# First cross-attention of a two-layer decoder: the totals of two chunk sums taken by TensorE's accumulation instead of by GpSimd

## The chip, the cores and the metric

The kernel runs on one core of a Trainium2 chip. The metric is the device time of one execution in microseconds (us), smaller is better. The profile names the engines PE (TensorE's matmuls), PEld (its weight loads), DVE (VectorE), ACT (ScalarE), POOL (GpSimd) and SP (SyncE, which issues the DMAs). All engines run their own instruction streams in order and meet at semaphores.

## The reference, cut to what matters

The whole program is a decoder of two layers (each: a mixer or self-attention, a cross-attention over a context, a feed-forward with experts), with a layer norm after each part. The change touches only the cross-attention of the first layer: 2 batch rows, 256 queries and 512 context rows each, 16 heads of 64.

```python
# inside _L0_xattn_ref: b = 2, n = 256, s = 512, HEADS = 16, DHEAD = 64
q = (lat @ Wq).reshape(b, n, HEADS, DHEAD).transpose(0, 2, 1, 3)
...
k = apply_rope(k, cos[None, None], sin[None, None])
scale = DHEAD ** (-0.5)
attn = jnp.einsum('bhnd,bhsd->bhns', q, k) * scale
attn = jnp.clip(attn, -11.0, 11.0)
attn = jax.nn.softmax(attn, axis=-1)
out = jnp.einsum('bhns,bhsd->bhnd', attn, v)
out = out.transpose(0, 2, 1, 3).reshape(b, n, INNER)
return out @ Wo + bo
```

So each head and query needs a denominator: the sum over 512 context rows of the clipped exponentials.

## The kernel before, in words

The attention is worked off in 16 entries p = 2c + b, where c (0 to 7) is a pair of heads and b (0 or 1) a batch row. In an entry, context rows lie on the partitions; they come as 4 tiles of 128, taken two at a time, so an entry has two chunks s = 0 and 1, numbered n = 4c + 2b + s (32 in all). The logits of a chunk fill two PSUM banks (128 x 1024); ScalarE takes the exponential (L907) into one of four places `ex(n)`, VectorE clips it in place (L1298, `e0_clip`), and then two engines read it: TensorE multiplies it with the values (`mix0`, into the left half of bank 4 + b, `e0_used`) and GpSimd adds the two context tiles of the chunk (L703) into `esum[:, s, :]` (`e0_sum`). After the second chunk GpSimd adds the two sums into `etot[:, b, :]` (L710, `e0_tot`). `denominators0` on TensorE multiplies the total with a block of ones, two products of 64 columns by 256, one for each head of the pair, into the right half of bank 4 + b, which adds over the partitions (`o0_ps`). VectorE takes the reciprocal of it (L1290) and multiplies (L1291, `o0_norm`).

The order is written out by hand. In iteration p, TensorE does a projection (and, for b = 0, one half of a later key product; for b = 1 only the other half), then the logits of entry p + 1, the mix of entry p, and the denominators of entry p - 1. On VectorE, the two clips of an entry stand ahead of the reciprocal of the entry two before (`normed0(c - 1, b)`), then, for b = 1, the two products of a rotary step (L1236). On GpSimd the sums of an entry stand ahead of its total, and after b = 1 comes `rotated0` (L664), which finishes keys that TensorE needs some entries later. The waits that matter: the mix of entry p waits for `o0_norm` of entry p - 2 (same PSUM half), ScalarE's exponential of chunk n waits for `e0_used` and `e0_sum` of chunk n - 4 (same place in `ex`), GpSimd's first sum of an entry waits for the total before (`e0_tot`, since `esum` has one place for each s), and GpSimd's total waits for `o0_ps` of the entry two before (since `etot` has one place for each b). The last chunk (n = 31) has no sum on GpSimd: `last_denominators0` reads `esum` and the exponentials themselves.

All matmuls go through the helper `mm`, so they all stand on L1676; the tile names tell them apart (`ps<-big` is the denominators, and in the first entries the logits; `ps<-big,late` the mix, `ps<-big,mid` the logits from entry 3 on). Each float32 product shows as two records in the profile.

Of the kernel before, what the change touches and what calls it, by code (L numbers as in the profile page):

```python
# [25 lines left out]
B, T = 2, 256  # L26
# [45 lines left out]
def program(nc, a, out):  # L72
    f32, bf16, u8 = mybir.dt.float32, mybir.dt.bfloat16, mybir.dt.uint8
    ALU, ACT, AX = mybir.AluOpType, mybir.ActivationFunctionType, mybir.AxisListType
    ctx = ExitStack()
    with ctx:
# [3 lines left out]
        def sem(name):  # L80
            return ctx.enter_context(nc.semaphore(name))
# [65 lines left out]
        def rv4(name):  # L147
# [48 lines left out]
        ones_sb = big2(3700, [P, PARTS * H * B * CS // P], bf16)  # L196
        ones_col = sb("ones_col", [P, 1])
        half_x = [big1(4096 * half, [P, 4096])[64:P] for half in range(2)]
        late_hidden, first_hidden = big1(2048, [P, 2048])[64:P], big1(0, [P, 2048])[64:P]
        cxT = ctx_r(2048, [P, B * CS])  # L200
# [9 lines left out]
        esum = big2(1536, [P, 2, 2 * T])  # L210
        etot = big2(2560, [P, 2, 2 * T])
        ones0 = big2(3584, [P, DH0])
# [43 lines left out]
        ps = ctx.enter_context(nc.psum_tensor("ps", [P, 8, 512], f32))  # L256
# [30 lines left out]
        S = {k: sem(k) for k in (  # L287
            "w1_ps", "v1_ps", "x1p_done", "conv_done", "xc_done", "gate_done",
            "dt_ps", "z_done", "BC_ps", "BC_done", "lg_done", "delta_parts", "dx_parts",
            "delta_done", "delta_rest", "second_quads", "late_quads",  # L290
            "spread_d", "spread_x", "dA_done", "dBx_done", "scan_done", "hC_done", "y_ps",
            "yv_done", "mo_ps", "res_ready", "x2_done", "ff_ps", "ff_act", "ff2_ps",
            "cxnT_ps", "cxnT_done",
            "k0_ps", "k0_mul", "k0_done", "q0_ps", "q0_done", "v0_ps", "v0_done", "s0_ps", "e0_exp",
            "e0_clip", "e0_used", "e0_sum", "e0_tot", "o0_ps", "o0_norm", "y0_ps",
# [120 lines left out]
        def before_in_bank(L, slot):  # L416

            placed = placed_slots(L)
            at = [s for _, s, _ in placed].index(slot)
            same = [s for n, s, bank in placed[:at] if bank == placed[at][2]]  # L420
            return same[-1] if same else None
# [61 lines left out]
        def ex(n):  # L483

            return ex_last if n % 4 == 3 else ex_first[:, n % 4, :]

        def half(t, b):

            return t[:, b * NJ // B:(b + 1) * NJ // B, :].rearrange("p j d -> p (j d)")
# [32 lines left out]
        def stack_x(sp, half):  # L522

            heads = slice(HB * half, HB * half + HB)
            sp.wait_ge(S[f"x_zero{half}"], 2 - half)
            for c in range(PARTS * PARTS):
                sp.dma_start(ks["x"][DH * c:DH * c + DH, heads, :],
                             scr_kx[P // 2 * half:P // 2 * half + P // 2, c // PARTS, :]
                             .rearrange("(h d) t -> d h t", d=DH)).then_inc(S["x_stack"], 16)
            sp.dma_start(ks["x"][STACK:ROWS, heads, :], ones_rows[:, heads, :]  # L530
                         ).then_inc(S["x_stack"], 16)
# [84 lines left out]
        def _(pool):  # L616
# [43 lines left out]
            def rotated0(n):  # L660

                c, b = divmod(n, B)
                pool.wait_ge(S["k0_mul"], 2 * n + 2)
                nc.gpsimd.tensor_tensor(kT0[c][:, b * CS:(b + 1) * CS], kt1[n % 2], kt2[n % 2],  # L664
                                        ALU.add).then_inc(S["k0_done"], 1)
# [27 lines left out]
            for n in range(4 * NPAIR):  # L693
                c, u = divmod(n, 4)
                b, s = divmod(u, 2)

                if n == 4 * NPAIR - 1:
                    continue
                pool.wait_ge(S["e0_clip"], n + 1)
                if n >= 2:  # L700
                    pool.wait_ge(S["e0_tot"], 2 * c + b)
                e = ex(n).rearrange("p (r k t) -> p r k t", r=2, k=2)
                nc.gpsimd.tensor_tensor(esum[:, s, :].rearrange("p (r t) -> p r t", r=2),  # L703
                                        e[:, :, 0, :], e[:, :, 1, :], ALU.add
                                        ).then_inc(S["e0_sum"], 1)
                if s == 1:
                    pool.wait_ge(S["e0_sum"], n + 1)
                    if c:
                        pool.wait_ge(S["o0_ps"], 2 * (c - 1) + b + 1)
                    nc.gpsimd.tensor_tensor(etot[:, b, :], esum[:, 0, :], esum[:, 1, :], ALU.add  # L710
                                            ).then_inc(S["e0_tot"], 1)
                if u == 3 and K_FIRST + c < B * NPAIR:
                    rotated0(K_FIRST + c)
            root("post1")
# [959 lines left out]
        def _(pe):  # L1674
            def mm(o, lhsT, rhs, start=True, stop=True, shared=False):
                return nc.tensor.matmul(o, lhsT, rhs, start=start, stop=stop, skip_group_check=shared)  # L1676
# [161 lines left out]

            def denominators0(c, b):

                pe.wait_ge(S["e0_tot"], 2 * c + b + 1)
                for r in range(2):
                    ins = mm(ps[64 * r:64 * r + 64, 4 + b, T:2 * T], ones0,
                             etot[:, b, r * T:(r + 1) * T], False, True, True)
                ins.then_inc(S["o0_ps"], 1)

            def last_denominators0(parts):

                n, b = 4 * NPAIR - 1, B - 1
                pe.wait_ge(S["e0_sum"], n)  # L1850
                for part in parts:
                    for r in range(2):
                        rhs = (esum[:, 0, r * T:(r + 1) * T] if part == 0 else
                               ex(n)[:, r * 512 + (part - 1) * T:r * 512 + part * T])
                        ins = mm(ps[64 * r:64 * r + 64, 4 + b, T:2 * T], ones0, rhs, False, part == 2, True)
                return ins
# [17 lines left out]
            for p in range(B * NPAIR):  # L1874
                c, b = divmod(p, B)
# [13 lines left out]
                if p + 1 < B * NPAIR:  # L1889
                    pe.wait_ge(S["k0_done"], p + 2)  # L1890
                    if b:
                        pe.wait_ge(S["q0_done"], c + 2)
                    logits0(2 * p + 2)
                    logits0(2 * p + 3)
                    mix0(2 * p)
                    mix0(2 * p + 1)
                    if p:
                        denominators0(*divmod(p - 1, B))
                else:
                    output0(2)  # L1900
                    output0(3)
                    denominators0(c, 0)
                    output0(4)
                    mix0(2 * p)
                    last_denominators0((0,))
                    mix0(2 * p + 1)
                    last_denominators0((1, 2)).then_inc(S["o0_ps"], 1)
# [14 lines left out]
            for i in range(2):  # L1922
                for k in range(4):
                    t = 4 * i + k
                    ins = mm(ps[:, 7 - 4 * i, k * P:(k + 1) * P], cxT[:, t * P:(t + 1) * P],
                             w_x1[:, 2, :])
# [8 lines left out]
            for j in range(NJ):  # L1935
                ins = mm(ps[:, 4, j * E0:(j + 1) * E0], xT[:, j * P:(j + 1) * P], w_r0[:])
# [566 lines left out]
```

## Time and profile before

| | us |
|---|---|
| median of 3 timed runs | 450.51 (449.87 to 451.18) |
| the profiled execution, whole time | 447.8 |
| its span (first to last instruction) | 446.0 |
| of the span, PE busy | 407.5 |
| DVE busy | 303.2 |
| ACT busy | 205.1 |
| POOL busy | 196.5 |

The first cross-attention's entries lie between about 88 and 185 us of the span. A row of the timeline gives the start, the duration, the engine, the source line, what is written and read, and how many instructions are merged; an idle time ahead of it stands in brackets with what ended it. The chain of work that ended last follows back from the last instruction to whatever released each step.

### The profile page before, as it was taken

The page shows a single profiled execution, that of the slowest core. Times are in us where ns is not written, and L with a number is a line of the kernel's source. Part 1 is how long each engine was busy: PE and PEld are TensorE (multiplying, and loading weights), DVE is VectorE, ACT ScalarE, POOL GpSimd, SP SyncE. Part 2 cuts the span into 40 slices and gives each one's busy share as a digit, 9 for nine tenths or more (in the row PEclk, how much of TensorE's full clock was granted, in tenths as well). Part 3 has the DMA queues.
Part 4 walks back from the last instruction along what each step waited for, and adds up shares of the span by engine and source line. Part 5 has one row for each costly group of instructions (what it writes and reads, how often), then busy time and mean ns, then how long its engine had stood idle before and what let it go on. Part 6 is the DMA issues. An engine that isn't in the chain of part 4 may idle for free.

```text
span 446.0 us, 7698 instructions
## 1 busy us (share of the span) xinstructions
PE 407.5 (91%) x2882; PEld 275.8 (62%) x2882; DVE 303.2 (68%) x688; ACT 205.1 (46%) x290; POOL 196.5 (44%) x237
## 2 busy tenths in 40 slices
PE   4898999999999999989999986799779999999985
PEld 4576644455555557747898764445555555558974
DVE  4779976768988888624424978573798894355654
ACT  1676633154333333242333476457256545557550
POOL 3316657699988887050322556212453233000000
PEclk9989999999999999999999998899999999999999
DMA  8812000000005111350251015100000000010000
GB/s 299 320 33 85 2 1 1 1 1 0 1 0 190 48 47 48 100 193 1 103 77 22 2 31 69 15 3 3 0 2 3 2 3 2 2 37 1 0 1 24
DMA packets 8080, 19.78 MB, mean 44 GB/s; under 512 B 1958, under 2 KB 3974, under 8 KB 7526
## 3 DMA queue, kind: packets, MB, share of 16 engines
q1 hardware_dynamic: 8044, 19.30, 14.6%
q8 instruction: 23, 0.38, 0.3%
q14 instruction: 13, 0.11, 0.1%
HBM read 17.26 MB, written 1.15 MB: 41 GB/s over the span
## 4 chain that ended last, share of the span: by engine, by line
PE 72%; DVE 14%; DMA 5%; issue 3%; POOL 3%; ACT 3%; SPq 0%; DVEq 0%; POOLq 0%; ACTq 0%
PE ps L1676 70%; DMA late<-mid 4%; DVE ps L1421 3%; DVE big L1227 2%; DVE ps L1222 2%; DVE mx_a L1425 1%; PE ps L1688 1%; DMA ident<-in_ident 1%; DVE big L1298 1%; POOL rstd L638 1%; POOL big L657 1%; PE ps L2150 1%; PE ps L2073 0%; ACT late L1073 0%; DVE mid L1451 0%
## 5 line engine op out<-in xcount | busy, mean ns | idle before, releaser
L1676 PE MATMUL ps<-big,late 128*32 128x256 f32 (+3 forms) x768 | 96.1, 380 | 3.2 <-DVE mx_a L1425 1.5
L967 ACT ACTIVATE big<-ps 128x1024 f32<-128x1024 f32 x48 | 49.0, 1023 | 39.5 <-PE ps L1676 39.3
L1676 PE MATMUL ps<-late,big 128*128 128x128 f32 (+1 forms) x448 | 65.6, 277 | 1.5 <-DMA late<-mid 1.5
L1676 PEld LDWEIGHTS ps<-big,late 128*32 128x32 f32 (+2 forms) x768 | 36.7, 116 | 38.1 <-issue 14.9
L1676 PEld LDWEIGHTS ps<-late,big 128*128 128x128 f32 (+1 forms) x448 | 47.2, 152 | 19.7 <-issue 12.9
L636 POOL TENSOR_SCALAR vareps<-meanvar 128x2 f32<-128x2 f32 (+2 forms) x13 | 2.9, 226 | 110.0 <-DVE meanvar L1121 106.2
L907 ACT ACTIVATE big<-ps 128x1024 f32<-128x1024 f32 x32 | 31.0, 1022 | 38.9 <-PE ps L1676 37.5
L1421 DVE CUSTOM_DVE_ANT_0 ps<-ps,big 128x512 f32<-128x512 f32 x64 | 42.7, 708 | 6.9 <-PE ps L1676 5.8
L703 POOL TENSOR_TENSOR big<-big 128x512 f32<-128x512 f32 x31 | 43.8, 1428 | 5.5 <-DVE big L1298 5.3
L1298 DVE TENSOR_SCALAR big<-big 128x1024 f32<-128x1024 f32 x32 | 36.4, 1159 | 13.2 <-ACT big L907 12.8
L929 ACT ACTIVATE big<-ps 128x512 f32<-128x512 f32 x32 | 19.1, 597 | 36.7 <-PE ps L1676 36.7
L1676 PE MATMUL ps<-ident 128*128 128x128 f32 x182 | 27.5, 296 | 5.9 <-DMA ident<-in_ident 5.8
L1676 PE MATMUL ps<-ctx_r,attn_w 128*128 128x512 f32 x64 | 31.8, 607 | 0.7 <-ACT late L874 0.7
L1676 PEld LDWEIGHTS ps<-ident 128*128 128x128 f32 x182 | 25.5, 211 | 7.4 <-DMA ident<-in_ident 5.8
L1290 DVE RECIPROCAL big<-ps 128x256 f32<-128x256 f32 x16 | 28.0, 1748 | 3.0 <-PE ps L1676 3.0
L1676 PE MATMUL ps<-attn_w,ctx_r 128*128 128x128 f32 (+1 forms) x192 | 29.6, 288 | 0.3 <-ACT late L980 0.3
L1676 PE MATMUL ps<-xT,late 128*128 128x256 f32 (+1 forms) x96 | 29.6, 451 | 0.0
L657 POOL TENSOR_TENSOR big<-big,mid 128x512 f32<-128x512 f32 x16 | 20.4, 1273 | 19.5 <-DVE big L1227 19.5
L1676 PEld LDWEIGHTS ps<-attn_w,ctx_r 128*128 128x128 f32 (+1 forms) x192 | 23.8, 170 | 7.7 <-issue 2.9
L755 POOL CAST mid<-mid 4x256 bf16<-4x256 f32 (+1 forms) x12 | 4.6, 387 | 50.5 <-ACT mid L1023 50.4
L1425 DVE TENSOR_REDUCE mx_a<-ps 128x2 f32<-128x512 f32 x32 | 20.4, 685 | 8.8 <-PE ps L1676 8.8
L1676 PE MATMUL ps<-attn_w,big 128*128 128x128 f32 x192 | 25.4, 278 | 0.6 <-DVE big L1633 0.6
(261 smaller groups left out, 754.4 us busy)
## 6 DMA issues: line engine op xcount, KB each, us to landing
attn_w<-in_w_x SPq DMA_DIRECT2D x1, 2560.0 KB, 13.6
big<-parts_kx SPq DMA_DIRECT2D x18, 128.0 KB
late<-in_w_up SPq DMA_DIRECT2D x1, 2048.0 KB, 7.8
late<-in_w_dn SPq DMA_DIRECT2D x4, 512.0 KB, 3.8
attn_w<-in_w_up SPq DMA_DIRECT2D x1, 1024.0 KB, 7.9
attn_w<-in_w_dn SPq DMA_DIRECT2D x1, 1024.0 KB, 10.1
big<-mid SPq DMA_DIRECT2D x24, 32.0 KB, 1.8
parts_kx<-ctx_r SPq DMA_DIRECT2D x1, 768.0 KB, 3.2
```

The costliest lines, as they stand in the source:

```text
L657: nc.gpsimd.tensor_tensor(hC[:, s % 8, :], hs[:, s % 4, :], Cn[:], ALU.mult).then_inc(S["hC_done"], 1)
L703: nc.gpsimd.tensor_tensor(esum[:, s, :].rearrange("p (r t) -> p r t", r=2), e[:, :, 0, :], e[:, :, 1, :], ALU.add).then_inc(S["e0_sum"], 1)
L907: nc.scalar.activation(ex(n).rearrange("p (r n) -> p r n", r=2), ps[:, 2 * (n % 2):2 * (n % 2) + 2, :], ACT.Exp).then_inc(S["e0_exp"], 1)
L929: nc.scalar.activation(dst, ps[:, up_bank0(k, c), :], ACT.Gelu).then_inc(S["up0_act"], 1)
L967: nc.scalar.activation(ex1[:, n % 3, :].rearrange("p (r n) -> p r n", r=2), ps[:, 2 * (n % 2):2 * (n % 2) + 2, :], ACT.Exp, scale=scale).t ...
L1222: nc.vector.tensor_tensor(dBx, dBx, Bn[:], ALU.mult).then_inc(S["dBx_done"], 1)
L1227: nc.vector.tensor_tensor_scan(hs[:, s % 4, :], dA[:, s % 2, :], dBx, 0.0, ALU.mult, ALU.add).then_inc(S["scan_done"], 1)
L1290: link(nc.vector.reciprocal(dst, ps[:, 4 + b, T:2 * T]))
L1298: nc.vector.tensor_scalar(ex(n), ex(n), float(np.exp(CLIP)), float(np.exp(-CLIP)), ALU.min, ALU.max).then_inc(S["e0_clip"], 1)
L1421: nc.vector.tensor_tensor_reduce(ps[:, bank, :], ps[:, bank, :], mq[:, 2 * b + q, :], 1.0, -FAR, ALU.add, ALU.max, dst).then_inc(S[f"{L}_r ...
L1425: nc.vector.tensor_reduce(dst, ps[:, bank, :].rearrange("p (h k) -> p h k", h=heads), AX.X, ALU.max).then_inc(S[f"{L}_redmax"], 1)
L1676: return nc.tensor.matmul(o, lhsT, rhs, start=start, stop=stop, skip_group_check=shared)
```

## The change

GpSimd makes no totals any more. The two arrays `esum` and `etot` become one place of two sums for each batch row: entry (c, b) writes its sum s to `esum[:, s, :]` when b = 0 and to `etot[:, s, :]` when b = 1 (the helper `sums0`). GpSimd's sums wait for `o0_ps` of the entry two before in place of `e0_tot`, both sums of an entry and not the total alone. `denominators0` waits for `e0_sum` in place of `e0_tot`, and issues four products in place of two: it accumulates the two sums in PSUM. The last entry's handling only changes the name of the place.

```diff
+        def sums0(b, s):
+
+            return (esum, etot)[b][:, s, :]
...
                 pool.wait_ge(S["e0_clip"], n + 1)
-                if n >= 2:
-                    pool.wait_ge(S["e0_tot"], 2 * c + b)
+                if c:
+                    pool.wait_ge(S["o0_ps"], 2 * (c - 1) + b + 1)
                 e = ex(n).rearrange("p (r k t) -> p r k t", r=2, k=2)
-                nc.gpsimd.tensor_tensor(esum[:, s, :].rearrange("p (r t) -> p r t", r=2),
+                nc.gpsimd.tensor_tensor(sums0(b, s).rearrange("p (r t) -> p r t", r=2),
                                         e[:, :, 0, :], e[:, :, 1, :], ALU.add
                                         ).then_inc(S["e0_sum"], 1)
-                if s == 1:
-                    pool.wait_ge(S["e0_sum"], n + 1)
-                    if c:
-                        pool.wait_ge(S["o0_ps"], 2 * (c - 1) + b + 1)
-                    nc.gpsimd.tensor_tensor(etot[:, b, :], esum[:, 0, :], esum[:, 1, :], ALU.add
-                                            ).then_inc(S["e0_tot"], 1)
...
             def denominators0(c, b):
 
-                pe.wait_ge(S["e0_tot"], 2 * c + b + 1)
-                for r in range(2):
-                    ins = mm(ps[64 * r:64 * r + 64, 4 + b, T:2 * T], ones0,
-                             etot[:, b, r * T:(r + 1) * T], False, True, True)
+                pe.wait_ge(S["e0_sum"], 4 * c + 2 * b + 2)
+                for s in range(2):
+                    for r in range(2):
+                        ins = mm(ps[64 * r:64 * r + 64, 4 + b, T:2 * T], ones0,
+                                 sums0(b, s)[:, r * T:(r + 1) * T], False, s == 1, True)
                 ins.then_inc(S["o0_ps"], 1)
```

TensorE's stream in the middle of the attention, before: the mix of an entry (`big,late`), the denominators of the entry before (`big`), the key product, and the next logits.

```order
180 L1676 MATMUL ps<-big,late 64x256 [waits e0_clip]
181 L1676 MATMUL ps<-big,late 64x256 x3
182 L1676 MATMUL ps<-big 64x256 [waits e0_tot]
183 L1676 MATMUL ps<-big 64x256
184 L1676 MATMUL ps<-ctx_r,attn_w 128x512 [waits q0_done]
185 L1676 MATMUL ps<-big,mid 128x256 [waits e0_exp,q0_done,k0_done]
```

And the same stretch now:

```order
180 L1674 MATMUL ps<-big,late 64x256 [waits e0_clip]
181 L1674 MATMUL ps<-big,late 64x256 x3
182 L1674 MATMUL ps<-big 64x256 [waits e0_sum]
183 L1674 MATMUL ps<-big 64x256 x3
184 L1674 MATMUL ps<-ctx_r,attn_w 128x512 [waits q0_done]
185 L1674 MATMUL ps<-big,mid 128x256 [waits e0_exp,q0_done,k0_done]
```

Nothing is moved on TensorE; the denominators are four products where they were two, and wait for another semaphore.

GpSimd's stream in the entries of one pair of heads, before (L703 the sums, L710 the totals, L664 the rotary step):

```order
50 L703 TENSOR_TENSOR big<-big 128x512 [waits e0_tot,e0_clip] x2
51 L710 TENSOR_TENSOR big<-big 128x512 [waits o0_ps,e0_sum]
52 L703 TENSOR_TENSOR big<-big 128x512 [waits e0_tot,e0_clip] x2
53 L710 TENSOR_TENSOR big<-big 128x512 [waits o0_ps,e0_sum]
54 L664 TENSOR_TENSOR mid<-dtmp 128x512 [waits k0_mul]
```

And now (L707 the sums, L668 the rotary step), from the rotary step ahead of them:

```order
46 L668 TENSOR_TENSOR mid<-dtmp,big 128x512 [waits k0_mul]
47 L707 TENSOR_TENSOR big<-big 128x512 [waits o0_ps,e0_clip] x4
48 L668 TENSOR_TENSOR mid<-dtmp 128x512 [waits k0_mul]
49 L707 TENSOR_TENSOR big<-big 128x512 [waits o0_ps,e0_clip] x4
50 L668 TENSOR_TENSOR mid<-dtmp,big 128x512 [waits k0_mul]
```

The totals are gone, the four sums of a pair stand in one run, and each now waits for `o0_ps`, which the totals alone did.

## Rows read from the trace of the kernel before

**Rows 1.** The page: span, busy time of each engine.
```profile
span 446.0 us, 7698 instructions
PE 407.5 (91%) x2882; PEld 275.8 (62%) x2882; DVE 303.2 (68%) x688; ACT 205.1 (46%) x290; POOL 196.5 (44%) x237
```
**Rows 2.** Chain that ended last, in order of time, 88 to 187 us.
```profile
87.85 15.94 PE ps L1676 x102
...
103.81 1.03 ACT big L907
...
104.87 3.28 DVE big L1298 x2
108.16 1.68 DVE big L1290
...
109.86 0.43 DVE big L1291
...
110.42 76.39 PE ps L1676 x544
```
**Rows 3.** Who waited for whom: engine PE, 88 to 187 us.
```profile
PE ps L1676 <- DVE big L1291: 0.5, 1, 0.5
```
**Rows 4.** Groups by line and shape, 90 to 186 us.
```profile
L703 POOL TENSOR_TENSOR big<-big 128x512 f32<-128x512 f32 x31 | 43.8, 1428 | 5.5 <-DVE big L1298 5.3
L1298 DVE TENSOR_SCALAR big<-big 128x1024 f32<-128x1024 f32 x32 | 36.4, 1159 | 13.2 <-ACT big L907 12.8
L1290 DVE RECIPROCAL big<-ps 128x256 f32<-128x256 f32 x16 | 28.0, 1748 | 3.0 <-PE ps L1676 3.0
L710 POOL TENSOR_TENSOR big<-big 128x512 f32<-128x512 f32 x15 | 20.1, 1339 | 1.2
```
**Rows 5.** Timeline of PE, the last entries, 180 to 184 us.
```profile
180.74 0.60 PE L1676 MATMUL ps<-big 128*64 128x256 f32 x4
181.17 1.03 PE L1676 MATMUL ps<-big,late 128*64 128x256 f32 x8
182.03 1.03 PE L1676 MATMUL ps<-big 128*64 128x256 f32 x8
183.00 1.27 PE L1676 MATMUL ps<-attn_w,big 128*128 128x128 f32 x9
```
**Rows 6.** Timeline of all engines, one short iteration, 164 to 168 us.
```profile
164.13 0.60 PE L1676 MATMUL ps<-big 128*64 128x256 f32 x4
164.66 1.12 PE L1676 MATMUL ps<-ctx_r,attn_w 128*128 128x512 f32 x2
164.78 1.76 DVE L1290 RECIPROCAL big<-ps 128x256 f32<-128x256 f32 x1 [0.51 <-PE ps L1676]
165.72 2.00 PE L1676 MATMUL ps<-big,mid 64*128 64x256 f32 x16
166.57 0.42 DVE L1291 TENSOR_TENSOR big<-ps,big 128x256 f32<-128x256 f32 x1
...
167.65 0.65 PE L1676 MATMUL ps<-big,late 128*64 128x256 f32 x4
```
**Rows 7.** One line's instructions: the clips (ns: min/median/max).
```profile
L1298 DVE TENSOR_SCALAR big<-big x32: 679/1005/1802, 90.5 to 175.1; 128x1024 f32<-128x1024 f32 x32
```
**Rows 8.** Timeline of all engines, another short iteration, 151 to 156 us.
```profile
151.99 1.27 POOL L703 TENSOR_TENSOR big<-big 128x512 f32<-128x512 f32 x1 [0.70 <-DVE big L1298]
152.14 1.67 DVE L1298 TENSOR_SCALAR big<-big 128x1024 f32<-128x1024 f32 x1 [0.22 <-ACT big L907]
152.69 0.60 PE L1676 MATMUL ps<-big 128*64 128x256 f32 x4
...
153.89 1.26 POOL L703 TENSOR_TENSOR big<-big 128x512 f32<-128x512 f32 x1 [0.63 <-DVE big L1298]
...
155.23 1.27 POOL L710 TENSOR_TENSOR big<-big 128x512 f32<-128x512 f32 x1
```
**Rows 9.** Timeline of all engines: next exponentials, next denominators; last sum (162 to 176 us).
```profile
161.61 1.94 ACT L907 ACTIVATE big<-ps 128x1024 f32<-128x1024 f32 x2 [1.34 <-PE ps L1676]
...
174.95 1.28 POOL L703 TENSOR_TENSOR big<-big 128x512 f32<-128x512 f32 x1 [0.78 <-DVE big L1298]
...
175.64 0.60 PE L1676 MATMUL ps<-big 128*64 128x256 f32 x4
```
**Rows 10.** Stretches: engines' busy us, granted clock (PEclk), DMA share, GB/s.
```profile
270.00:275.00 5.00, 3.29 (x20) 2.18 (x21) 3.70 (x9) 3.83 (x5) 4.38 (x11) 0.84 0.54 66
285.00:290.00 5.00, 4.07 (x32) 2.08 (x34) 3.10 (x6) 2.95 (x3) 1.71 (x2) 0.79 0.01 2
```

More of the change, by code:

```diff
@@ L1852, in last_denominators0 @@
                     for r in range(2):
-                        rhs = (esum[:, 0, r * T:(r + 1) * T] if part == 0 else
+                        rhs = (sums0(b, 0)[:, r * T:(r + 1) * T] if part == 0 else
                                ex(n)[:, r * 512 + (part - 1) * T:r * 512 + part * T])
```

## The prediction

> **What bounds the kernel now.** I read the page first: TensorE is busy 407.5 of 446.0 us, VectorE 303.2, GpSimd 196.5 [rows 1]. That share alone says little about one stage, so the next view is the chain of work that ended last, cut to the stage that the change touches. It runs on TensorE for 15.94 us, goes once over ScalarE and VectorE (an exponential, two clips, a reciprocal and a product, from 103.81 to 110.29), and then stays on TensorE without a break for 76.39 us [rows 2]. The reader is to see there that no GpSimd line stands in the chain at all. The view of who waited for whom says the same from the other side: between 88 and 187 us TensorE was held up once, for 0.5 us, by the normalising product on VectorE [rows 3]. GpSimd is busy here with 31 sums (43.8 us) and 15 totals (20.1 us), VectorE with clips and reciprocals, and both have idle time before their work [rows 4]. So in this stage TensorE is the bound, up to half a microsecond.
>
> **The change part by part.**
>
> *Removed: 15 totals on GpSimd*, 20.1 us of its time [rows 4]. Their cover is TensorE's stream, which never waited for GpSimd [rows 3], so by themselves they give nothing back. What they give indirectly is VectorE's time. The clip takes 0.68 us at best and 1.16 us on average, up to 1.80 [rows 4, 7]; the slow ones lie beside GpSimd's work: the clip that starts at 152.14, inside a sum that runs from 151.99 to 153.26, takes 1.67 us and ends after it [rows 8]. In the stretch where the chain leaves TensorE the two clips take 3.28 us together [rows 2] where two free ones would take 1.4. There the reciprocal is reached at 108.16, late, and TensorE's mix waits 0.5 us for its product. With no totals GpSimd is less far behind in those first entries, the clips end earlier, and this wait goes: **-0.5 us**. What is late next there is TensorE itself, so no more than the 0.5 can come.
>
> *Added: two products in each `denominators0`.* It is called 15 times (entries 0 to 14; the last entry has its own function, whose products don't change), so 30 products, 60 records. The trace has this very operation at both sizes. A call of 4 records starts at 164.13 and the next product at 164.66, 0.53 us later [rows 6]. The call of the last entry has 8 records, the size that every call will have: it starts at 182.03 and the next product at 183.00, 0.97 us later [rows 5]. The difference is 0.44 us. A second reading: 4 records between two others of the same tile shape go from 180.74 to 181.17, 0.43 us, and 8 records of the mix from 181.17 to 182.03, 0.86 us [rows 5]. I take 0.435 x 15 = **+6.5 us**. The ends: the two readings give 6.45 to 6.6; if each added pair cost as much as a whole call with its change of tile shape (0.53), 15 x 0.53 = 8.0. All of it lies on TensorE's stream, and there is no idle time in which it could hide beyond the 0.5 already counted [rows 3]. That the products now accumulate, so that the third adds to what the first has written, is how the mix already works, and its 0.86 us for 8 records show no price for it.
>
> *Changed: what TensorE waits for.* `e0_sum` of the entry's second chunk comes one total earlier than `e0_tot` did, on the same engine. No cost.
>
> *Added: GpSimd's sums wait for `o0_ps` of the entry two before.* This wait is real. The sum at 151.99 would write the place that the denominators starting at 152.69 read [rows 8], as the places are after the change. Those complete 0.65 us after their start, as the reciprocal that waits for them shows (164.13 to 164.78) [rows 6], and 0.44 us later with the two more products: at 152.69 + 0.65 + 0.44 = 153.8. So the first sum starts 1.8 us later. Behind it are queued the second sum and, after each second entry, the rotary step. But the second sum can then follow at once, and the pair is done at 153.8 + 2 x 1.3 = 156.4, where the total before ended at 155.23 + 1.27 = 156.5 [rows 8]. GpSimd ends its entry no later than before. Who waits for the sums: ScalarE's exponentials into the same places, two entries after 150, thus at 161.61 [rows 9], 5 us later; and TensorE's denominators of the same entry, two iterations on, at 164.13 [rows 6], 7.7 us later. At the end of the stage the last sum, now at 174.95, would wait for the denominators that start at 175.64 [rows 9]: 175.64 + 1.09 + 1.3 = 178.0, and is asked for at 180.74 [rows 5]. All covered, by 2.7 us at the tightest: cost **0**, and the later half of the range if I am wrong (below). A side effect is that the sums now start with the reciprocal instead of beside the clips, so the clips should fall to about 0.7 us each.
>
> *The loop that is nearest to the path.* `o0_ps` comes 0.44 us later after the start of the denominators, and the mix of the next iteration waits for the reciprocal and the product behind it. In the short iteration VectorE is ready at 166.57 + 0.42 = 166.99, and the mix starts at 167.65; with about 0.14 us for the release, as at 109.86 + 0.43 to 110.42 [rows 2], 0.5 us is left. TensorE's own path to that mix grows by the same 0.44 us, so the slack stays 0.5. Cost 0.
>
> *Sum.* +6.5 - 0.5 = **+6.0 us**. Against the profiled execution: 447.8 + 6.0 = 453.8 us, with a span of 452.0. The timed runs of the same kernel have a median 2.7 us above the profiled one, and I carry this distance over: 450.51 + 6.0 = **456.5 us**, 1.3% slower. Everything after 187 us follows TensorE's last products of the stage and moves by the same 6 us; loads of weights start relative to the same events or earlier.
>
> *What the sum leaves out: TensorE's clock.* The granted clock is 0.84 and 0.79 in two stretches long after this stage, where TensorE has gaps [rows 10]; that is full speed with about a fifth to a third of the 5 us at the lower of its two levels. Where such a stretch falls relative to the gaps can move when all is shifted by 6 us. A period of it costs (1 - 0.79) x 5 = 1 us or so, and could come or go: ±1.5 us in the range, nothing in the sum.
>
> **The rivals.**
>
> *Faster: VectorE and GpSimd set the pace, not TensorE.* The clips sum to 36.4 us, and 32 at 0.69 us would be 22.1, so up to 14.3 us of VectorE's time comes free, with 20.1 us of GpSimd's [rows 4, 7]. If VectorE's loop (clip, reciprocal, product, mix) were the bound in all entries and TensorE's records only looked busy, the stage would shrink by up to this: 450.5 - 14.3 = 436 us. It begins to beat the old time once TensorE's hidden waits exceed 6.5 us. The iterations speak against it: apart from the one wait TensorE is never held up in the stage [rows 3], and its products follow each other at their own length. Chance 0.03. The Trainium skill, "SBUF — State Buffer", section "Who interferes with whom", says that GpSimd and a VectorE instruction in its two-port mode exclude each other for the whole instruction, whichever came first. The clip at 152.14 [rows 8] agrees in that the clip outlasts the sum by half a microsecond; by this rule the freed VectorE time would be the gain that the change is made for, and only the chain [rows 2] says that it buys nothing.
>
> *No change: the added products hide.* TensorE leaves about 0.1 us at each change of tile shape (0.53 against 0.43) [rows 5, 6]. If the two products fitted into waits that the profile doesn't show, only the -0.5 would be left: 450.0 us. Against it: the call with 8 records costs its full 0.97. Chance 0.03.
>
> *Slower than forecast: the new wait closes a loop.* GpSimd's sums wait for TensorE's denominators, these wait for the mix, this for VectorE's reciprocal. If the slack of 0.5 us in the short iterations is not there (a reciprocal or a product slowed by a sum that now starts at the same moment, by 1 us say), TensorE waits 0.5 us in each of 7 or 8 of them: +4 us, 460.5 us. The reciprocal's mean of 1748 ns with GpSimd at work beside it speaks against that [rows 4]. Chance 0.06.
>
> **How the numbers follow.** Forecast 456.5 us, chance 0.88. Its own bounds: 6.4 to 8.0 for the products, 0 to 0.5 for the wait that goes, ±1.5 for the clock, and the runs' own spread of 0.7. Together, not all at once, 454.6 to 458.4, which leaves under 2 in 10 outside with the rivals. A measurement of this kernel can tell about 0.3%, 1.35 us, from no change. Faster by more than that: 0.03. Within it: 0.03. Slower: 0.94.
>
> **What the profile of the changed kernel would show.** Right: 15 groups of 8 denominators' records, each 0.97 us from its start to the next product, and 60 more records on TensorE; GpSimd's busy time down by some 20 us; clips near 0.7 us; sums that begin with the reciprocals; no wait of TensorE for `o0_norm` in the stage, which gets some 6 us longer; the rest of the span as it was. Wrong: TensorE waiting for L1291 in each short iteration (the third rival), or iterations that are as long as before although there are more products (the first two). If the stage grows by 6 us and the time doesn't, the later stages gave it back, and my claim that they merely shift is what failed.

## The result and the profile after

The changed kernel takes 456.47 us (median of 4 runs, 454.62 to 457.61) against 450.19 us of the kernel before, a ratio of 1.0133 with a 95% interval of 1.0095 to 1.0171 (estimated from all runs; the two medians alone divide to 1.014). The forecast was 456.5 us. The profiled execution took 456.17 us with a span of 454.4 us. One run of experiment 1 below (454.87 us) fell in a slower state of the chip and is left out of its median.

The page of the changed kernel, span and engines (before: [rows 1]):

```profile
span 454.4 us, 7788 instructions
PE 415.4 (91%) x2942; PEld 280.0 (62%) x2942; DVE 297.8 (66%) x688; ACT 205.2 (45%) x290; POOL 172.3 (38%) x222
```

TensorE has 60 records more, the 30 added products, and GpSimd 15 instructions fewer. GpSimd's busy time fell by 24 us and VectorE's by 5, and yet the kernel is slower.

The chain that ended last, changed kernel, in order of time over the stage (before: [rows 2]):

```profile
85.41 107.71 PE ps L1674 x758
...
193.14 0.70 DVE summed L1258
```

The chain no longer leaves TensorE: the excursion over the clips and the reciprocal that stood at 103.81 to 110.29 is gone, and the view of waits has no row for TensorE in the stage. To compare kernels I use the *stage length*: from the start of the first logits (the first row below) to the start of the addition behind the stage (`summed`). Before it is 186.84 - 87.78 = 99.06 us, now 193.14 - 88.18 = 104.96 us: 5.90 us more, where the prediction had 6.0.

A short iteration of the changed kernel, timeline of all engines but the weight loads, from the first logits and then 142 to 150 us (before: [rows 6], [rows 8]):

```profile
88.18 2.00 PE L1674 MATMUL ps<-big 64*128 64x256 f32 x16
...
142.62 0.69 DVE L1296 TENSOR_SCALAR big<-big 128x1024 f32<-128x1024 f32 x1 [1.82 <-ACT big L905]
143.54 0.69 DVE L1296 TENSOR_SCALAR big<-big 128x1024 f32<-128x1024 f32 x1 [0.22 <-ACT big L905]
...
144.09 1.03 PE L1674 MATMUL ps<-big 128*64 128x256 f32 x8
145.05 1.13 PE L1674 MATMUL ps<-ctx_r,attn_w 128*128 128x512 f32 x2
145.17 1.76 DVE L1288 RECIPROCAL big<-ps 128x256 f32<-128x256 f32 x1 [0.94 <-PE ps L1674]
145.28 2.49 POOL L707 TENSOR_TENSOR big<-big 128x512 f32<-128x512 f32 x2 [4.09 <-PE ps L1674]
146.11 2.00 PE L1674 MATMUL ps<-big,mid 64*128 64x256 f32 x16
146.96 0.42 DVE L1289 TENSOR_TENSOR big<-ps,big 128x256 f32<-128x256 f32 x1
...
148.04 1.95 PE L1674 MATMUL ps<-big,late 128*64 128x256 f32 x16
148.50 2.36 DVE L1296 TENSOR_SCALAR big<-big 128x1024 f32<-128x1024 f32 x2
148.66 1.65 POOL L668 TENSOR_TENSOR mid<-dtmp,big 128x512 f32<-128x512 f32 x1 [0.89 <-DVE big L1234]
```

The denominators' call now has 8 records and lasts 0.96 us from its start to the next product (144.09 to 145.05). The reciprocal starts 1.08 us after the call's start, as worked out (0.65 + 0.44). GpSimd waits 4.09 us for the denominators, and its two sums start right behind them. VectorE's product ends at 147.38 and the mix follows at 148.04, so the slack is again about 0.5 us after the release.

Groups by line and shape of the changed kernel, 90 to 192 us (before: [rows 4]):

```profile
L707 POOL TENSOR_TENSOR big<-big 128x512 f32<-128x512 f32 x31 | 39.5, 1297 | 34.3 <-PE ps L1674 30.8 <-DVE big L1296 3.5
L1296 DVE TENSOR_SCALAR big<-big 128x1024 f32<-128x1024 f32 x32 | 29.5, 925 | 18.2 <-ACT big L905 17.6
L1288 DVE RECIPROCAL big<-ps 128x256 f32<-128x256 f32 x16 | 28.1, 1758 | 9.8 <-PE ps L1674 9.6
```

GpSimd has 34 us of idle time before its sums where it had 5.5, almost all of it behind the new wait. VectorE has 18.2 and 9.8 us before clips and reciprocals where it had 13.2 and 3.0. Both got time that nobody asked for.

The span grew by 8.4 us, not 5.9. The stage starts 0.40 us later (88.18 against 87.78), and behind it come 2.1 us more (261.26 against 259.16). Of these, 1.7 us lie in one place. Stretches of the changed kernel from 199 us, 1 us each (columns as in [rows 10]), and TensorE's timeline up to the first expert products (`ps<-xT,late`), changed kernel first, kernel before second:

```profile
199.00:200.00 1.00, 1.00 (x9) 1.00 (x10) 0.00 (x0) 0.00 (x0) 0.00 (x0) 1.00 0.84 319
200.00:201.00 1.00, 1.00 (x2) 0.42 (x2) 0.85 (x8) 0.00 (x0) 0.00 (x0) 0.61 1.01 401
201.00:202.00 1.00, 1.00 (x2) 0.34 (x1) 0.66 (x8) 0.49 (x1) 0.20 (x1) 0.50 0.72 303
```
```profile
197.19 1.00 PE L1686 MATMUL ps<-ident,x 128*128 128x128 f32 x4 [0.55 <-DVE x L1129]
198.93 1.03 PE L1674 MATMUL ps<-w_r,xT 128*128 128x8 f32 x8 [0.73 <-issue]
199.81 4.52 PE L1674 MATMUL ps<-xT,late 128*128 128x512 f32 x6
```
```profile
193.51 2.82 PE L1676 MATMUL ps<-xT,late 128*128 128x512 f32 x6
```

TensorE's granted clock fell to the lower of its two levels (0.50, that is 1.2 GHz) soon after 200 us, behind two short gaps of TensorE (0.55 and 0.73 us; the kernel before has the same two and no fall there), and six records took 4.52 us where they had taken 2.82: 1.7 us.

### The profile page after: what moved, and what is told of

Read it like the earlier page. It is cut to its first block, busy times and chain, and to the rows that moved or that the text cites. A ratio compares the mean times of both kernels' runs of the same rounds, so it can differ in the third digit from the quotient of the medians.

```text
span 454.4 us, 7788 instructions
## 1 busy us (share of the span) xinstructions
PE 415.4 (91%) x2942; PEld 280.0 (62%) x2942; DVE 297.8 (66%) x688; ACT 205.2 (45%) x290; POOL 172.3 (38%) x222
## 3 DMA queue, kind: packets, MB, share of 16 engines
HBM read 17.26 MB, written 1.15 MB: 41 GB/s over the span
## 4 chain that ended last, share of the span: by engine, by line
PE 74%; DVE 13%; ACT 3%; POOL 3%; issue 3%; DMA 2%; SPq 1%; DVEq 0%; POOLq 0%; ACTq 0%
PE ps L1674 71%; DVE ps L1419 2%; DVE mx_a L1423 2%; DVE big L1225 1%; SPq L567 1%; DMA ident<-in_ident 1%; DVE ps L1220 1%; DMA big<-mid 1%; POOL big L741 1%; PE ps L1686 1%; PE ps L2072 1%; POOL rstd L642 1%; POOL big L661 1%; PE ps L2149 1%; ACT late L1071 0%
## 5 line engine op out<-in xcount | busy, mean ns | idle before, releaser
L1674 PEld LDWEIGHTS ps<-big,late 128*32 128x32 f32 (+2 forms) x768 | 36.4, 116 | 37.3 <-issue 14.4
L707 POOL TENSOR_TENSOR big<-big 128x512 f32<-128x512 f32 x31 | 39.5, 1297 | 34.3 <-PE ps L1674 30.8
L1296 DVE TENSOR_SCALAR big<-big 128x1024 f32<-128x1024 f32 x32 | 29.5, 925 | 18.2 <-ACT big L905 17.6
L1674 PE MATMUL ps<-ident 128*128 128x128 f32 x182 | 28.6, 303 | 6.7 <-DMA ident<-in_ident 6.7
L1674 PEld LDWEIGHTS ps<-ident 128*128 128x128 f32 x182 | 26.5, 218 | 8.4 <-DMA ident<-in_ident 6.7
L1674 PE MATMUL ps<-xT,late 128*128 128x256 f32 (+1 forms) x96 | 31.3, 471 | 0.0
L1674 PE MATMUL ps<-xT,attn_w 128*128 128x256 f32 (+1 forms) x80 | 25.1, 432 | 0.9 <-ACT xT L815 0.9
L1674 PEld LDWEIGHTS ps<-attn_w,big 128*128 128x128 f32 x192 | 23.6, 191 | 3.6 <-issue 1.7
```

The lines of the kernel that those rows point to most:

```text
L707: nc.gpsimd.tensor_tensor(sums0(b, s).rearrange("p (r t) -> p r t", r=2), e[:, :, 0, :], e[:, :, 1, :], ALU.add).then_inc(S["e0_sum"], 1)
L1296: nc.vector.tensor_scalar(ex(n), ex(n), float(np.exp(CLIP)), float(np.exp(-CLIP)), ALU.min, ALU.max).then_inc(S["e0_clip"], 1)
```

## The experiments

*Theory*: TensorE bounds the stage, each added pair of products costs its own 0.435 us, and all else is covered. *Rivals*: GpSimd's new wait, or the pace of VectorE, has a part in the price or could have given something back.

All times are medians. The ratio is to the kernel before, run on the same chip beside each (450.08 us beside experiments 1 to 4, 450.01 us beside the others). It is estimated from all runs, with its 95% interval in brackets, and can differ from the quotient of two medians by up to 0.003.

### 1. The added products taken away again, the waits kept

```diff
-                for s in range(2):
+                for s in range(1, 2):
                     for r in range(2):
                         ins = mm(ps[64 * r:64 * r + 64, 4 + b, T:2 * T], ones0,
```

> The changed kernel with the first of its two sums left out of the denominators (they cover only the second chunk of each entry): two products a call as before the change, no totals on GpSimd, and all the new waits as changed. Theory (the added products are the whole price, 0.435 us a call on TensorE's stream, and the totals' removal gives only the 0.5 us wait of the early entries): 456.5 - 6.5 = 450.0 us, and TensorE waits nowhere in the stage. Rival (the new wait of GpSimd's sums or the later reciprocals cost time): it stays above 452 us.

Measured: 448.85 us (9 runs), ratio 0.997 (0.9941 to 0.9999). The chain over the stage:

```profile
85.12 101.23 PE ps L1674 x698
186.37 0.70 DVE summed L1258
```

60 records fewer, 6.48 us shorter than the 107.71 us of the changed kernel: 0.432 us for each of the 15 calls. The stage length is 186.37 - 87.89 = 98.48 us, 0.58 under the kernel before. So the totals' removal and the new wait, taken together, are worth about half a microsecond, and in a chain that never leaves TensorE the new wait costs nothing.

### 2. The products doubled, GpSimd as before

```diff
-                for r in range(2):
-                    ins = mm(ps[64 * r:64 * r + 64, 4 + b, T:2 * T], ones0,
-                             etot[:, b, r * T:(r + 1) * T], False, True, True)
+                for s in range(2):
+                    for r in range(2):
+                        ins = mm(ps[64 * r:64 * r + 64, 4 + b, T:2 * T], ones0,
+                                 etot[:, b, r * T:(r + 1) * T], False, s == 1, True)
```

> The kernel before, with the two products of each total issued twice (denominators of entries 0 to 14 come out doubled): GpSimd and its totals are untouched. Theory: 15 x 0.435 = +6.5 us on 450.2, so 456.7 us; the iterations grow from 11.44 to 12.31 us for two entries. The early wait for the normalising product stays near 0.5 us, since both sides of it shift. Rival (part of the price of the change is in its waits): under 455 us.

Measured: 456.28 us, ratio 1.0143 (1.0091 to 1.0195). The chain and the clips:

```profile
84.69 107.71 PE ps L1676 x758
192.42 0.70 DVE summed L1260
```
```profile
L1298 DVE TENSOR_SCALAR big<-big 128x1024 f32<-128x1024 f32 x32 | 37.1, 1167 | 17.7 <-ACT big L907 17.1
```

The chain on TensorE is 107.71 us, equal to the changed kernel's to the hundredth, though GpSimd makes its totals and the clips are as slow as ever. The stage is 192.42 - 87.47 = 104.95 us. One thing was missed: the early wait for the normalising product, which was to stay at 0.5 us, is gone here too. With a longer TensorE stream VectorE and GpSimd are in time in the first entries too, with all their totals.

### 3. GpSimd's totals made again, for nobody

```diff
+        unread = big2(1024, [P, 2 * T])
...
                                         ).then_inc(S["e0_sum"], 1)
+                if s == 1:
+                    pool.wait_ge(S["e0_sum"], n + 1)
+                    nc.gpsimd.tensor_tensor(unread, sums0(b, 0), sums0(b, 1), ALU.add
+                                            ).then_inc(S["e0_tot"], 1)
+                    pool.wait_ge(S["e0_tot"], 2 * c + b + 1)
```

> The changed kernel with GpSimd still making each total, into a place that nothing reads: only the relief of GpSimd is taken back. Theory: 456.5 us to 457.0, since TensorE sets the pace and at most the wait of 0.5 us in the early entries comes back; clips are slowed again where a total lies beside them. Rival (VectorE's freed time counts): several us more, up to the 7 us that the clips have given back.

Measured: 454.49 us, ratio 1.011 (1.0067 to 1.0152), within the scatter of the changed kernel. Chain and clips:

```profile
85.06 107.71 PE ps L1680 x758
192.79 0.70 DVE summed L1264
```
```profile
L1302 DVE TENSOR_SCALAR big<-big 128x1024 f32<-128x1024 f32 x32 | 34.5, 1098 | 14.9 <-ACT big L911 14.8
```

The stage is 192.79 - 87.83 = 104.96 us. With the longer TensorE stream the 20.1 us of GpSimd's totals and the 5 us of VectorE's clips are worth 0.00 us.

### 4. GpSimd's sums with places of their own

```diff
+        sums_odd0 = big1(2048, [P, 2, 2 * T])
+        sums_odd1 = (big1(3072, [P, 2 * T]), big2(1024, [P, 2 * T]))
...
-            return (esum, etot)[b][:, s, :]
+            return (esum, etot)[b][:, s, :] if c % 2 == 0 else sums_odd1[s] if b else sums_odd0[:, s, :]
...
-                if c:
-                    pool.wait_ge(S["o0_ps"], 2 * (c - 1) + b + 1)
+                if c >= 2:
+                    pool.wait_ge(S["o0_ps"], 2 * (c - 2) + b + 1)
```

> The changed kernel with four places of sums in place of two, so that GpSimd's sums wait for the denominators four entries before, and no longer begin with the reciprocals. Theory (that wait is covered by 5 us): 456.5 us, no change; the sums start beside the clips again, and the clips go back towards 1 us. Rival (the wait holds something up): 455 us or less.

Measured: 457.4 us, ratio 1.0154 (1.0094 to 1.0213). Chain, sums and clips:

```profile
85.39 107.71 PE ps L1676 x758
193.12 0.70 DVE summed L1260
```
```profile
L709 POOL TENSOR_TENSOR big<-big 128x512 f32<-128x512 f32 x31 | 42.8, 1394 | 22.0 <-DVE big L1298 22.0
L1298 DVE TENSOR_SCALAR big<-big 128x1024 f32<-128x1024 f32 x32 | 36.4, 1141 | 18.2 <-ACT big L907 17.6
```

The sums now wait for the clips again (22.0 us) and not for TensorE, and the clips are slow again: 36.4 us for the 32, exactly as before the change [rows 4]. The stage is still 193.12 - 88.16 = 104.96 us. With the long TensorE stream the 32 clips now have four figures: 37.1 us with the totals and without the new wait (experiment 2), 36.4 without either, 34.5 with both (experiment 3), and 29.5 in the changed kernel, with the wait and without the totals. So the wait, which moves the sums behind the clips, had to come together with the missing totals: alone the one gives 2.6 us, the other 0.7, both 7.6. And neither matters to the end.

### 5. The changed kernel again

> The changed kernel once more, beside the three that follow: 456.5 us. In its first profile TensorE fell to its lower level at 200.4 us, just after the short gaps behind the attention, and the first expert products took 1.7 us longer than before the change. Theory (where such a fall comes is a matter of the execution, not of the change): another profile of the same kernel may show it elsewhere or not at all, with the attention's own stretch unchanged to 0.1 us. Rival (the change causes it): the same fall in the same place again.

Measured: 455.04 us (9 runs, 453.22 to 457.35), ratio 1.0104 (1.0068 to 1.014). The stage is 192.78 - 87.82 = 104.96 us. Stretches of this execution, and then the same stretches of the first one:

```profile
199.00:204.00 5.00, 5.00 (x17) 2.62 (x17) 1.50 (x15) 2.39 (x4) 2.56 (x1) 1.00 0.58 233
281.00:286.00 5.00, 4.45 (x27) 2.57 (x25) 4.42 (x8) 3.38 (x4) 2.12 (x6) 0.80 0.39 61
286.00:296.00 10.00, 7.40 (x54) 4.31 (x54) 4.74 (x8) 4.34 (x6) 3.31 (x5) 0.83 0.01 3
320.00:330.00 10.00, 7.67 (x45) 6.02 (x46) 7.33 (x22) 2.54 (x6) 5.73 (x12) 0.87 0.00 0
330.00:340.00 10.00, 7.41 (x43) 5.47 (x43) 8.24 (x25) 4.39 (x8) 4.80 (x12) 0.84 0.00 0
```
```profile
199.00:204.00 5.00, 5.00 (x14) 2.63 (x15) 1.50 (x15) 1.19 (x2) 2.20 (x1) 0.66 0.62 247
281.00:286.00 5.00, 4.80 (x26) 3.23 (x24) 3.11 (x7) 3.35 (x4) 3.93 (x10) 0.54 0.54 73
286.00:296.00 10.00, 6.99 (x57) 4.34 (x54) 5.79 (x10) 5.88 (x7) 3.32 (x5) 1.00 0.11 19
320.00:330.00 10.00, 7.37 (x50) 5.64 (x51) 7.48 (x25) 2.63 (x7) 5.22 (x12) 1.00 0.00 0
330.00:340.00 10.00, 7.41 (x44) 5.28 (x43) 8.81 (x27) 4.41 (x8) 5.82 (x14) 0.84 0.00 0
```

The same program, and the clock falls in other places: at full level behind the stage, and at the lower one for a part of two stretches where the first execution had none. So the change doesn't by itself bring the fall behind the stage. But the second execution didn't gain by that: the length of each of these five stretches times what its clock lacks to 1.00 adds up to 5.6 us in both, and behind the stage it took 455.0 - 192.78 = 262.22 us, more than the 261.26 of the first.

The scatter of 3 to 6 us between runs of one kernel goes with the clock. Of 22 runs of the kernel before, beside this one, the five with a mean granted clock of 0.983 took 448.75 us on average and the eight with 0.979 took 450.19. The profiled execution of the kernel before had 0.986, as only one of the 22 had: it was a fortunate one.

### 6. Totals in bfloat16, in the kernel before

```diff
-                    nc.gpsimd.tensor_tensor(etot[:, b, :], esum[:, 0, :], esum[:, 1, :], ALU.add
+                    nc.gpsimd.tensor_tensor(etoth[:, b, :], esum[:, 0, :], esum[:, 1, :], ALU.add
...
-                    ins = mm(ps[64 * r:64 * r + 64, 4 + b, T:2 * T], ones0,
-                             etot[:, b, r * T:(r + 1) * T], False, True, True)
+                    ins = mm(ps[64 * r:64 * r + 64, 4 + b, T:2 * T], ones0h,
+                             etoth[:, b, r * T:(r + 1) * T], False, True, True)
```

> The kernel before, with GpSimd's totals of entries 0 to 14 written as bfloat16 and multiplied with ones in bfloat16. A float32 product shows as two records; if one in bfloat16 of the same columns is one, the call's 0.43 us fall to 0.11 us or, with half the records at the same length, to 0.21. Theory (each 0.1 us of TensorE's time in a call is 1.5 us of the kernel): 450.2 - 15 x 0.32 = 445.4 us, or 446.9 with 0.21. Rival (the stage has another bound close behind TensorE, the reciprocals or the clips): 449 us or more.

Measured: 444.33 us, ratio 0.9879 (0.9831 to 0.9927). A call in the timeline of TensorE, and who TensorE waited for in the stage:

```profile
161.25 0.28 PE L1679 MATMUL ps<-big 128*64 128x256 bf16 x2
161.46 1.13 PE L1679 MATMUL ps<-ctx_r,attn_w 128*128 128x512 f32 x2
```
```profile
PE ps L1679 <- DVE big L1294: 0.8, 1, 0.8
```

A product is one record now, and the call takes 0.21 us where it took 0.53: 15 x 0.32 = 4.8 us less. The stage is 182.64 - 87.94 = 94.70 us, 4.36 less than before: the early wait grew from 0.5 to 0.8 us and takes 0.3 us of the gain back, and 0.1 us is not accounted for. The scale of the theory holds downwards too. It also shows where the other bound lies: with TensorE faster, the early entries start to wait for VectorE and GpSimd.

### 7. Sums in bfloat16, in the changed kernel

The helper `sums0` returns the places in bfloat16 and the ones follow:

```diff
-            return (esum, etot)[b][:, s, :]
+            return (esumh, etoth)[b][:, s, :]
...
-                        ins = mm(ps[64 * r:64 * r + 64, 4 + b, T:2 * T], ones0,
+                        ins = mm(ps[64 * r:64 * r + 64, 4 + b, T:2 * T], ones0h,
                                  sums0(b, s)[:, r * T:(r + 1) * T], False, s == 1, True)
```

> The changed kernel with GpSimd's sums in bfloat16: four products a call, in bfloat16, in all entries (of the last one only the part that reads a sum). Theory: a call costs 0.21 us in place of 0.87, so 456.5 - 15 x 0.65 = 446.7 us, or 450.0 if a bfloat16 product only halves. Against the kernel with bfloat16 totals it has 30 products more and 15 totals less: 15 x 0.11 us more, less the 0.5 us wait. Rival (another bound): 451 us or more.

Measured: 445.04 us, ratio 0.989 (0.9851 to 0.9928). The output of this kernel is off from the reference's by a relative error of 0.029, so it shows what the products cost and is not a kernel to use; how much of the error each rounding makes was not looked into.

```profile
161.36 0.39 PE L1678 MATMUL ps<-big 128*64 128x256 bf16 x4
161.68 1.12 PE L1678 MATMUL ps<-ctx_r,attn_w 128*128 128x512 f32 x2
```

The call takes 0.32 us, 0.11 more than with totals, and TensorE waits for nobody. The stage is 182.86 - 87.93 = 94.93 us. It differs from experiment 6 by 0.23 us: 15 x 0.11 = 1.6 us of products are nearly paid for by the wait with its surroundings and by the last entry's own product in bfloat16 (0.3 us). The former is about 1.0 us in experiment 6: experiment 1, which waits nowhere, less 15 x 0.32 us would be 98.48 - 4.8 = 93.7 us, and the stage has 94.70. Here, as in experiment 1, where TensorE's stream is short enough to wait for the other engines, the removed totals and the new wait buy something; which of the two does it was not separated.

### 8. TensorE's gaps behind the stage filled

```diff
-            idle_work(2, 4)
+            idle_work(2, 7)
             pe.wait_ge(S["kx_done"], 2)
             to_cols(0, x, "xT_ps", "post1")
+            idle_work(2, 4)
```

> The changed kernel with idle products of TensorE in the two gaps behind the attention: three more ahead of the transposes and four between the transposes and the router. Theory (the fall of the clock at 200.4 us follows the gaps): no fall within 10 us of them in its profile, and the median 0 to 1.7 us lower, as often as the fall had come, 455.5 us. Rival (the gaps have nothing to do with it, or the products get in the way): no change, or 0.5 us more.

Measured for the changed kernel: 453.89 us (8 runs), ratio 1.008 (1.0053 to 1.0107), 1.15 us under the changed kernel of experiment 5, with intervals that overlap. Its stage is 104.95 us, and the clock doesn't fall right behind it, but nor did it in experiment 5.

The same in the kernel before:

> The kernel before with the same two gaps filled. Theory (the gaps' fall of the clock comes in some executions of any of these kernels): 449.0 us, 1 us under the kernel before, as the filled version of the changed kernel lay 1.1 us under its own. Rival (the kernel before has no such fall, as its profile shows none at this place, so there is nothing to win): 450.1 us.

Measured: 447.43 us (12 runs), ratio 0.9956 (0.9929 to 0.9983).

And with experiment 6:

> The kernel before with the totals of entries 0 to 14 in bfloat16 and TensorE's gaps behind the attention filled with idle products (three more and four). Theory: the two gains are in different stretches and add up: 444.3 us of the bfloat16 totals alone less about 1, 443.3 us. Rival (the fall of the clock only moves to a later gap, where it costs the same): 444.3 us.

Measured: 443.77 us, ratio 0.9884 (0.9843 to 0.9925), which can't be told from 444.33 alone. The filling gives about half a percent in the kernel before.

The gain goes with the clock, and not only at the filled gaps. The profiled executions with the filling took 258.47 us (before), 258.95 (changed) and 259.10 (with experiment 6) from `summed` to the end of the span. Without it the kernel before took 259.16 and the eight other profiled executions 259.71 to 262.24, with or without a fall right behind the gaps: experiments 2 and 4 had one there, as the first execution of the changed kernel did, the others only later ones. The runs say the same: the median of their mean granted clocks is 0.9865 with the filling and 0.980 without it in the kernel before, 0.9875 and 0.983 in the changed one. The two gaps themselves cost nothing: from `summed` to the first expert product the filled kernel before takes 192.71 - 186.03 = 6.68 us, the unfilled one 193.51 - 186.84 = 6.67. Why the later falls become fewer as well is open.

### The stage lengths side by side

| kernel | GpSimd totals | records a call | stage us | median us |
|---|---|---|---|---|
| before | yes | 4 | 99.06 | 450.2 |
| changed | no | 8 | 104.96 | 456.5, again 455.0 |
| 1, one sum | no | 4 | 98.48 | 448.9 |
| 2, doubled | yes | 8 | 104.95 | 456.3 |
| 3, unread totals | yes | 8 | 104.96 | 454.5 |
| 4, own places | no | 8 | 104.96 | 457.4 |
| 6, totals in bfloat16 | yes | 2 | 94.70 | 444.3 |
| 7, sums in bfloat16 | no | 4, bfloat16 | 94.93 | 445.0 |

The changed kernel and the three variants with 8 records a call have the same stage to 0.01 us, and medians from 454.5 to 457.4, that is 4.4 to 7.3 us above the kernel before, on either side of the stage's 5.9. The stage is the sharp instrument here, the whole time a blunt one.

## Why the prediction was right

*Added products, +6.5 us.* Right. The call of 8 records that the trace of before already held, in the last entry (0.97 us), was the call that came (0.96 us); taking 15 pairs away in experiment 1 shortens the stage by 6.48 us, and adding them to the kernel before in experiment 2 lengthens it by 5.89 us, which is 6.48 less what the early wait gave back.

*The early wait, -0.5 us.* Right in size (the wait's row is gone; experiment 1 gives 0.58 with what surrounds it), but the reason was only half of it. The prediction tied it to the totals' removal. Experiment 2 keeps the totals and loses the wait as well, so a longer TensorE stream alone is enough. In the changed kernel both are present, and the wait would have gone either way. Nor was 0.5 the most that could come, as the prediction had it: with its surroundings it is 0.58.

*GpSimd's new wait, cost 0.* Right: 30.8 us of idle time behind it, and no one late. Experiment 4 takes most of the wait away, at no gain.

*The loop over the reciprocal, cost 0.* Right, the slack is 0.5 us as before.

*The clips near 0.7 us.* Half wrong. Their median is 0.69 us, their mean 0.92 (one line's instructions, ns, min/median/max):

```profile
L1296 DVE TENSOR_SCALAR big<-big x32: 679/694/1778, 90.9 to 180.5; 128x1024 f32<-128x1024 f32 x32
```

In the short iterations, where the sums used to run beside them, they are quick. In the others the two clips take 2.36 us together (148.50 above), for the rotary step on GpSimd still runs there (148.66); the prediction had forgotten this neighbour. It costs nothing.

*The rest of the span merely shifts.* True but for the clock. The fall behind the stage cost 1.7 us in the first profiled execution and was absent in the second; the ±1.5 us that stood in the range for it was about its size. The prediction had taken 1 us for one fall, from stretches that cut a fall in two, and had misread their clock: with a lower level of half speed, 0.84 and 0.79 mean that 0.32 and 0.42 of the 5 us ran at it, and not a fifth to a third.

*The profiled execution*, predicted at 453.8, took 456.17: 5.9 for the stage, 0.4 ahead of it and 2.1 behind it, the 1.7 of the clock among these. The profiled execution of before had been 2.4 to 2.7 us under its median, at a granted clock of 0.986, and that of the changed kernel, at 0.983, was only 0.3 us under its own. One cannot carry such a distance over as a property of the kernel. The 6.0 us added to the median stand on the mechanism; that the median was then met to 0.03 us is luck, as the second set of runs of the same kernel had 455.04.

*The rivals.* Faster by VectorE's freed time: it fell with experiments 3 and 4, which take 5 and 7 of those microseconds back at no cost. The Trainium skill says ("SBUF — State Buffer", "Who interferes with whom") that GpSimd and a VectorE instruction in its two-port mode exclude each other for the whole instruction. The clips fit that: they are quick where the sums start behind them (0.69 us at 142.62 and 143.54) and slow where a sum or the rotary step lies beside. What lies beside a clip decides the clip's length, and still not the kernel's time. Hidden products and a closed loop: neither occurred.

## What to carry to other kernels

Work taken off an engine that nobody waits for is worth nothing, and an operation handed from it to the engine that the chain runs on costs its full length: read the chain of the stage before moving work, not the shares of busy time. A special case in the same loop (here the last entry's call of 8 records) may already show the new operation at its new size. If the bounding engine makes a sum, look at its number format first: here bfloat16 for the totals alone saved 0.32 us a call and gave the fastest kernels of this study (443.8 and 444.3 us). What it costs in precision has to be looked at each time: with all sums in bfloat16 the output was off by 0.029.

## What the runs showed of the hardware that I had not expected

- Two more products of 256 columns that add onto the two before them cost 0.432 us a call (experiment 1), no more than the 0.43 of two that stand alone [rows 5]: adding into PSUM showed no price of its own.
- A bfloat16 product between float32 ones in the same PSUM bank costs no change of its own: 0.21 us a call of two, 0.32 us of four, 0.11 us for the added pair, a quarter of the float32 pair's 0.43.
- Executions of one program agree to 0.01 us in a stage where TensorE waits for nothing, and differ by 3 to 6 us over the whole, which goes with how often and where TensorE's granted clock falls (0.66 against 1.00 in the same 5 us of two executions; 448.75 against 450.19 us at mean clocks of 0.983 and 0.979).
